# Mixed expert slots of a half and two quarters in a post-norm attention and expert kernel

## The reference, cut to what matters

```python
x = layernorm(x + attn_block(x))       # 8 x 512 tokens of width 256: sparse linear, 16 heads, dense FFN
x = layernorm(x + expert_block(x))

def expert_block(x):                   # 8 experts, E x (256 -> 1024 -> 256), one expert a token
    aff = x @ centroids.T
    assign = argmax(aff, axis=1)
    alpha = sigmoid(aff[assign])
    h = relu(layernorm(x, ln_g[e], ln_b[e]) @ w1[e].T + b1[e])
    y = x + h @ w2[e].T + b2[e]        # e = assign of the token
    return alpha * y + (1 - alpha) * x
```

## Time and profile before

| | |
|---|---|
| median of 3 runs | 870.22 us (870.16 to 870.26) |
| the profiled execution | 868.88 us, of which the trace spans 867.1 us |
| PE busy | 849.4 us (98%) |
| DVE, ACT, POOL busy | 460.1 (53%), 338.2 (39%), 288.9 us (33%) |
| mean granted TensorE clock | 0.995 of 2.4 GHz |
| HBM read, written | 76.33 MB, 11.49 MB |

### The profile page before, as it was taken

One profiled execution on the slowest core, in us unless ns is written; L12 is line 12 of the kernel. 1 busy time (PEld: TensorE's weight loads), 2 busy tenths in 40 slices (PEclk: granted clock), 3 DMA queues, 4 the chain that ended last, 5 costly groups with the idle time before them and its releaser, 6 DMA issues.

```text
span 867.1 us, 19050 instructions
## 1 busy us (share of the span) xinstructions
PE 849.4 (98%) x7078; PEld 570.2 (66%) x7078; DVE 460.1 (53%) x1374; ACT 338.2 (39%) x650; POOL 288.9 (33%) x404
## 2 busy tenths in 40 slices
PE   8999999999999999999999999999999999999994
PEld 4545576476467467557557647779989767667673
DVE  5465355256257347346448526525785556556552
ACT  1443415424432432631532442414233545454540
POOL 3503021422242061061152133415555444444422
PEclk9999999999999999999999999999999999999998
DMA  6501100020020020020002104224638876767820
GB/s 245 183 3 31 43 2 1 26 74 1 26 74 1 26 73 2 26 74 1 27 26 99 50 1 135 99 74 149 208 126 289 284 254 232 264 235 245 287 76 12
DMA packets 37697, 88.53 MB, mean 102 GB/s; under 512 B 13411, under 2 KB 26596, under 8 KB 30310
## 3 DMA queue, kind: packets, MB, share of 16 engines
q1 hardware_dynamic: 32118, 75.40, 25.5%
q0 software_dynamic: 5056, 11.37, 4.1%
q10 hardware_dynamic: 432, 0.54, 0.2%
HBM read 76.33 MB, written 11.49 MB: 101 GB/s over the span
## 4 chain that ended last, share of the span: by engine, by line
PE 92%; DVE 4%; POOL 1%; issue 1%; ACT 1%; DMA 1%; POOLq 0%; DVEq 0%; ACTq 0%
PE ps L580 13%; PE ps L586 12%; PE ps L673 9%; PE ps L691 9%; PE ps L527 8%; PE ps L551 7%; PE ps L738 5%; PE ps L713 4%; PE ps L499 3%; PE ps L559 3%; PE ps L426 3%; PE ps L447 3%; PE ps L455 3%; PE ps L389 2%; PE ps L723 1%; PE ps L659 1%
## 5 line engine op out<-in xcount | busy, mean ns | idle before, releaser
L586 PE MATMUL ps<-ff2T,hT 128*128 128x256 f32 x512 | 121.0, 384 | 0.2 <-ACT hT L1479 0.2
L580 PE MATMUL ps<-xT,ff1T 128*128 128x512 f32 x256 | 118.8, 604 | 0.1
L1487 ACT ACTIVATE arena<-ps 128x1536 f32<-128x1536 f32 (+3 forms) x49 | 65.1, 1328 | 127.5 <-DVE arena L985 126.9
L586 PEld LDWEIGHTS ps<-ff2T,hT 128*128 128x128 f32 x512 | 94.3, 190 | 16.3 <-issue 3.4
L985 DVE SCALAR_TENSOR_TENSOR arena<-ps,arena 128x512 f32<-128x512 f32 (+4 forms) x59 | 44.9, 767 | 105.7 <-PE ps L527 63.2
L691 PE MATMUL ps<-w_sb,arena 128*128 x400 | 95.8, 383 | 0.0
L691 PEld LDWEIGHTS ps<-w_sb,arena 128*128 128x128 f32 x400 | 72.2, 190 | 17.3 <-issue 9.5
L580 PEld LDWEIGHTS ps<-xT,ff1T 128*128 128x128 f32 x256 | 45.6, 190 | 52.2 <-issue 47.9
L527 PE MATMUL ps<-arena 32*128 32x512 f32 (+7 forms) x896 | 73.0, 434 | 1.7 <-ACT hT L1004 1.2
L1557 ACT ACTIVATE arena<-ps,arena 128x128 f32<-128x128 f32 (+1 forms) x94 | 34.3, 429 | 98.5 <-PE ps L659 98.5
L1792 POOL DMA_INDIRECT out_y<-arena,ids x36 | 37.3, 1035 | 87.4 <-DVE arena L1281 80.1
(11 more groups left out here) (209 smaller groups left out, 1487.5 us busy)
## 6 DMA issues: line engine op xcount, KB each, us to landing
arena<-in_w SPq DMA_DIRECT2D x24, 1024.0 KB, 5.4
hT<-in_w SPq DMA_DIRECT2D x14, 1024.0 KB, 6.7
wts<-in_w SPq DMA_DIRECT2D x9, 1024.0 KB, 5.4
w_sb<-in_w SPq DMA_DIRECT2D x8, 1024.0 KB, 5.1
token_store<-x SPq DMA_DIRECT2D x8, 520.0 KB, 3.6
arena<-in_x SPq DMA_DIRECT2D x8, 512.0 KB, 3.9
arena<-in_epack SPq DMA_DIRECT2D x25, 134.0 KB, 3.6
slot_table<-padid POOLq DMA_DIRECT2D x4, 576.0 KB, 6.0
```

The lines of the kernel that those rows point to most:

```text
L580: last = eng.matmul(ps[:, 6 + m % 2, :], ff1T[:, kd, m * P:(m + 1) * P], xT3[:, kd, :], start=kd == 0, stop=kd == KD - 1)
L586: last = eng.matmul(quarter(6, t), hT[:, m, t * P:(t + 1) * P], ff2T[:, m, :], start=m == 0, stop=m == FM - 1)
L1487: eng.activation(o, i, ACT.Relu).then_inc(s_sa, 1)
```

## The change

Left-over rows are handed out in units of 64 and 32 instead of 64 alone. A mixed slot now has three parts: a half (64 rows) and two quarters (32 rows each), each of its own expert. With that the rows fit in 34 slots: the same 25 full ones and 9 mixed ones instead of 11. The mixed slots are 14, 16, 18, 21, 23, 25, 28, 30 and 32.

- PE: the layers of a mixed slot run in four column strips of 32 (the half's two strips read the same weights): 16 products instead of 8 in layer 1 and 32 instead of 16 in layer 2, each half as wide in its stationary operand.
- First weights: three ring buffers a mixed slot (3 MB) instead of two, in the same ring of six.
- Second weights: all three parts are copied by ACT (three copies of 128x2048 instead of one), in four fixed places in turn.
- Parameters: six DMAs for a mixed slot instead of four, ids three instead of two. `slot_act_x_T` has six operations instead of four.
- Hidden units of a mixed slot: DVE adds the biases for both halves of them with four broadcast operations, then ACT and DVE take one relu each, instead of eight operations on either engine.
- Tables: four instead of three, the last one built in step 9 of DVE; the first mixed ids wait for all four.
- SP's order in a step becomes: first weights of j, parameters of j, ids of j+3.
- Two pairs of SBUF tensors are laid side by side so that they can serve as weight copies.

```diff
-QT = P // 2
+QT = P // 4
 NQ = P // QT
+PART_ROWS = (slice(0, 2 * QT), slice(2 * QT, 3 * QT), slice(3 * QT, P))
+NP = len(PART_ROWS)
+PART_OF = (0, 0, 1, 2)
...
-MIXED = {j: (j - N_EARLY) // 2 for j in range(N_EARLY + 1, N_TILE, 2)}
+MIXED = {N_EARLY + i: (i + 1) * N_MIX // N_LATE for i in range(N_LATE) if (i + 2) * N_MIX // N_LATE > (i + 1) * N_MIX // N_LATE}
...
-N_TAB = (N_EARLY, N_FULL - N_EARLY, NQ * N_MIX)
+N_TAB = (N_EARLY, N_FULL - N_EARLY, N_MIX, 2 * N_MIX)
+UNIT = (P, P, 2 * QT, QT)
...
-            w1_of[j] = [queue.pop(0) for _ in range(NQ if j in MIXED else 1)]
+            w1_of[j] = [queue.pop(0) for _ in range(NP if j in MIXED else 1)]
...
 # mixed_pe_layer1
                     for q in range(NQ):
-                        last = eng.matmul(ps[half_rows(q), b0 + i, :], sxT[u][:, kd, half_rows(q)],
-                                          w1_ring[w1_of[j][q]][:, c:c + S], start=kd == 0, stop=kd == KD - 1,
+                        last = eng.matmul(ps[quarter_rows(q), b0 + i, :], sxT[u][:, kd, quarter_rows(q)],
+                                          w1_ring[w1_of[j][PART_OF[q]]][:, c:c + S], start=kd == 0, stop=kd == KD - 1,
...
 # mixed_pe_layer2
-            eng.wait_ge(m_w2, MIXED[j] + 1)
+            eng.wait_ge(m_w2, NP * (MIXED[j] + 1))
...
 # mixed_dve_hidden
+            for k, (turned, done) in enumerate(((m_Ta, m_add), (m_Tb, m_add2))):
+                eng.wait_ge(turned, i + 1)
...
+                eng.tensor_tensor(shT[u][:, f, 0:2 * QT], src[:, :, 0:2 * QT], c[:, e].unsqueeze(2).broadcast_to([P, 4, 2 * QT]),
+                                  ALU.add)
+                eng.tensor_tensor(shT[u][:, f, 2 * QT:P].rearrange("p f (q c) -> p f q c", c=QT),
+                                  src[:, :, 2 * QT:P].rearrange("p f (q c) -> p f q c", c=QT),
+                                  quarters[:, e, :].unsqueeze(3).broadcast_to([P, 4, NP - 1, QT]), ALU.add).then_inc(done, 1)
+            eng.wait_ge(m_add2, i + 1)
+            eng.tensor_scalar(shT[u][:, 4:FM, :], shT[u][:, 4:FM, :], 0.0, None, ALU.max).then_inc(p_hTd, 1)
...
 # dve_program
                 if j == 8:
                     dve_find_experts(eng, 2)
                     dve_slot_table(eng, 2)
+                    dve_count_tiles(eng, 3)
+                if j == 9:
+                    dve_place_tiles(eng, 3)
+                    dve_find_experts(eng, 3)
+                    dve_slot_table(eng, 3)
...
 # act_program
-                if j == N_EARLY:
-                    mixed_act_second_weights(eng, 0)
-                if j in MIXED and MIXED[j] + 1 < N_MIX:
-                    mixed_act_second_weights(eng, MIXED[j] + 1)
+                if j in MIXED:
+                    mixed_act_weights(eng, NP * MIXED[j] + 1)
+                elif j == N_EARLY or j - 1 in MIXED and MIXED[j - 1] + 1 < N_MIX:
+                    mixed_act_weights(eng, NP * (MIXED[j - 1] + 1) if j - 1 in MIXED else 0)
...
                 if j + 1 < N_TILE:
                     slot_act_norm(eng, j + 1)
+                if j in MIXED:
+                    mixed_act_weights(eng, NP * MIXED[j] + 2)
...
 # slot_sp_ids
             if MIXED[j] == 0:
-                eng.wait_ge(s_tab, 3)
+                eng.wait_ge(s_tab, len(N_TAB))
...
 # sp_program
-                if XN <= j + 3 < N_TILE:
-                    slot_sp_ids(eng, j + 3)
                 slot_sp_w1(eng, j)
                 slot_sp_ep(eng, j)
+                if XN <= j + 3 < N_TILE:
+                    slot_sp_ids(eng, j + 3)
```

More of the change, by code:

```diff
@@ L375, in turn_of, with quarter_rows, columns_of @@
             return 16 * sum(parts if i in MIXED else 1 for i in range(j % ring, j + 1, ring))
-        def half_rows(q):
+        def quarter_rows(q):
             return slice(q * QT, (q + 1) * QT)
+        def columns_of(part):
+            return EW + 12 * (part - 1) if part else 0
         def pe_keep_warm(eng, bank, count):
@@ L704, in mixed_pe_layer1 @@
             u, b0 = j % UN, 2 * (j % 2)
-            for q in range(NQ):
-                eng.wait_ge(s_w1[w1_of[j][q]], turn_w1[j][q])
+            for p in range(NP):
+                eng.wait_ge(s_w1[w1_of[j][p]], turn_w1[j][p])
             eng.wait_ge(p_xTe, j + 1)
@@ L1552, in slot_act_x_T @@
                 eng.wait_ge(p_l1d, j - UN + 1)
-            for q, rows in enumerate([half_rows(q) for q in range(NQ)] if j in MIXED else [slice(0, P)]):
+            for p, rows in enumerate(PART_ROWS if j in MIXED else (slice(0, P),)):
                 for kd in range(KD):
-                    g, b = q * EW + E_G + kd, q * EW + E_B + kd
+                    g, b = columns_of(p) + E_G + kd, columns_of(p) + E_B + kd
                     last = eng.activation(sxT[u][:, kd, rows], ps[:, 6, kd * P + rows.start:kd * P + rows.stop], ACT.Identity,
@@ L1905, in slot_sp_ids @@
             if MIXED[j] == 0:
-                eng.wait_ge(s_tab, 3)
-            for q in range(NQ):
-                at = half_entry(eng, j, q, 1, NE * N_TOK)
-                eng.dma_start(ids[half_rows(q), j:j + 1], places[bass.ds(at, QT), 0:1],
+                eng.wait_ge(s_tab, len(N_TAB))
+            for p, rows in enumerate(PART_ROWS):
+                at = part_entry(eng, j, p, 1, NE * N_TOK)
+                eng.dma_start(ids[rows, j:j + 1], places[bass.ds(at, rows.stop - rows.start), 0:1],
                               allow_slow_non_contiguous=True).then_inc(d_ids[j % XN], 16)
@@ L1920, in slot_sp_ep @@
                 return
-            for q in range(NQ):
-                row = half_entry(eng, j, q, 2, (NE - 1) * P)
-                eng.dma_start(ep[j % EN][:, q * EW:q * EW + 12], epack[bass.ds(row, P), 0:12],
+            for p, rows in enumerate(PART_ROWS):
+                row, c = part_entry(eng, j, p, 2, (NE - 1) * P), columns_of(p)
+                eng.dma_start(ep[j % EN][:, c:c + 12], epack[bass.ds(row, P), 0:12],
                               allow_slow_non_contiguous=True).then_inc(d_ep[j % EN], 16)
-                eng.dma_start(ep[j % EN][half_rows(q), E_B2:E_B2 + H],
-                              epack[bass.ds(row, QT), E_B2:E_B2 + H]).then_inc(d_ep[j % EN], 16)
+                eng.dma_start(ep[j % EN][rows, E_B2:E_B2 + H],
+                              epack[bass.ds(row, rows.stop - rows.start), E_B2:E_B2 + H]).then_inc(d_ep[j % EN], 16)
         def slot_sp_w1(eng, j):
@@ L1945, in slot_sp_w1 @@
                     eng.wait_ge(s_f2, 2 * NB)
-            for q, u in enumerate(w1_of[j]):
-                row = half_entry(eng, j, q, 2, (NE - 1) * P) if j in MIXED else slot_entry(eng, j, 2, (NE - 1) * P)
+            for p, u in enumerate(w1_of[j]):
+                row = part_entry(eng, j, p, 2, (NE - 1) * P) if j in MIXED else slot_entry(eng, j, 2, (NE - 1) * P)
                 eng.dma_start(w1_ring[u], w1[bass.ds(row, P), :]).then_inc(s_w1[u], 16)
```

153 lines of the change are left out of this document (84 added, 69 removed).

## The result

The changed kernel takes 895.64 us (median of 4 runs, 894.93 to 896.92) beside 870.19 for the kernel before on the same chip: 1.0294 times, with a 95% interval of 1.0277 to 1.0312. The prediction was 865.9 with a range up to 874.5, so both the value and the sign were wrong. The profiled execution spans 893.5 us against 867.1, and the difference of 26.4 us is what has to be explained. Some 1.3 us of it lie between executions and not between kernels, since the profiled execution of the kernel before took 868.88 us, 1.3 under the median of 870.22.

The account below looks back on a forecast made before the run. PE, busy 98%, was taken to bound the kernel: 867.1 - 17.24 + 0.5 + 10.2 + 0.3 + 1.9 = 862.8 us of span, and with 3.1 to the median 865.9 us; 8-in-10 range 856.5 to 874.5.

Parts of the forecast that it names:

- Two slots: PE's path: two mixed slots go at 8.62 us each, 17.24 us off, while the 25 full slots stay.
- Four strips: Mixed slots' layers on PE: four strips run side by side, 0.05 us a slot more, 0.5 us for nine.
- Which slots wait: PE before layer 1: 16, 18, 23, 25, 30 and 32 wait for first weights and parameters, no other mixed slot.
- The wait's size: PE before layer 1: parameters land at 12.0 us, layer 1 starts near 14.2 against 12.44; 1.7 us in six slots, 10.2.
- the second rival: DMA queue before layer 1: loads run at 3.65 us each, waits of 3.1 us a slot, 874.3 us; chance 0.2.
- s: PE's wait before layer 1 in each of the six waiting slots: 1.7 us expected, bounds 1.0 and 3.1.
- The clock: PE in the expert slots: granted clock already at the 2.4 GHz level, so nothing to be had from it.
- 855.7 + 6 s: Whole kernel's time in us, with s as the wait of each of six slots; breaks even at s = 2.4.
- The tables: DVE's table building up to step 9: later normalisation and late first mixed ids, 1.9 us more, bounds 0.6 and 4.
- Who else stands behind this: POOL's gather and DVE's normalisation behind the later ids of j+3: hidden by some 2 us, no cost.
- x_T: ACT's `slot_act_x_T` before layer 1: six operations take 1.77 us; 0.3 us for three mixed slots without the long wait.
- ACT and DVE: Mixed slots: some 3 us more ACT work a pair, DVE within 1 us; both cost 0, bounds 0 and 0.5 a slot.

## Why the prediction was wrong, step by step

- **Two slots, -17.24.** Right: in the version with a wait for each buffer the waits before layer 1 are 6.9 us, its layers 1 take 4.5 us more than 9 x 3.43, and the tables cost 2.6; with two slots saved that gives 867.1 - 17.24 + 6.9 + 4.5 + 2.6 = 863.9 us, and 1.3 for the execution, against a span of 865.6. Without them it could not be under the kernel before.
- **Four strips, +0.5.** Right in kind, short in size: 0.12 us a slot, 1.1 for nine, all of it in layer 1.
- **Which slots wait.** The six named do, 21 and 28 don't. Slot 14 was missed: the distance of its buffers is four slots, but at the start a backlog of other weights and table waits stands before it on SP. I looked at the ring and not at SP's order there, although the rows of 655 to 671 showed that backlog. 3.9 us, and 1.7 more for its slow layer (5.34 against 3.64). With the backlog taken away the wait was 0.34.
- **The wait's size, six times 1.7.** This is the step that failed. PE's work between (12.42 us against 12.44), the starts of SP's issues and ACT's 1.77 were right within 0.2 us. The landing was not. The third load was to land at 11.6 and the parameters 0.4 behind. The forecast took 2.9 us a load from the mean rate of the DMA engines, and that mean was right: 361 GB/s in the window shown, 1.05 MB in 2.9 us. But landings aren't means. The third load landed 11.6 us after the first issue and not 10.7 (the run with parameters first), one parameter DMA behind it landed at 13.2 and not 12.0, and six of them another 1.2 later. From the 4.9 us of a load alone to 11.6 for the third are 3.35 us a load, between the 2.9 taken and the 3.65 of the earlier trace rows, which stood in the prediction as the bound and as the second rival's; I set it aside since gathers shared that window. The 1.2 us for six DMAs stood nowhere.
- **Where the second rival falls short.** It named the mechanism and s = 3.1, and gave 874.3. The waits were 3.45. The other 20 us are mostly the next point and slot 14.
- **The clock.** The prediction read 1.00 in the kernel before and took it that "nothing is to be had from it". There was something to lose. With forecast waits of 1.7 us little might have been lost: in the run with one parameter DMA, waits of 1.72, 1.86, 2.10 and 2.34 us left layer 1 at 3.64. But 2.24 and 2.52 gave 5.34 there, 2.00 gave 5.37 in the run with half the bytes, and in all runs 3 to 6 us gave 4.9 to 6.5. In the kernel after, layer 1 has 44.86 us against 9 x 3.64 = 32.8 at the upper level: 12.1 us for the clock and 1.9 for the strips and for starting behind a wait. The time is not 855.7 + 6 s; somewhere between s of 1.9 and 2.4 each slot adds nearly 2 us at once, just below where the sum breaks even (2.4), so that the second rival should have been priced some 10 us higher (six times 5.34 less 3.64).
- **The tables, +1.9.** 3.1 us by their two waits, or 2.6 more than the 0.5 of the earlier trace rows, inside the bounds of 0.6 to 4.
- **Who else stands behind this, x_T, ACT and DVE.** POOL's 11.9 us stay covered, and the ids' order costs nothing there. No row has PE waiting for copies of second weights in the kernel after.

Put together: 862.8 forecast; 10.5 for the six waits, 3.9 for slot 14, 13.5 for layer 1 (14.0 less the 0.5), 0.7 for the tables and 0.4 for slots 21 and 28 make 891.8, and with the 1.3 between executions 893.1, against a span of 893.5. Of the 29.8 us between the forecast of 865.9 and the measured 895.64, some 21 follow from the one step, the landing: 10.5 of longer waits and 10.4 of the lower clock behind them. Slot 14 has another 5.6.

**What stays open.** What holds a landing back beyond the bytes. The rate of a backlog read by landings was 3.35 to 3.65 us a load, by bytes 2.9. The packets of the kernel after in the two half microseconds from 702 on give a hint: few bytes in many small packets on the queue.

```profile
DMA packets 310, 0.11 MB, mean 230 GB/s; under 512 B 242, under 2 KB 305, under 8 KB 305
...
DMA packets 235, 0.05 MB, mean 94 GB/s; under 512 B 207, under 2 KB 233, under 8 KB 233
```

These are mostly the parameters, and they take the engines a microsecond for 0.16 MB. But the run that took away 336 of their 384 rows of 48 bytes saved nothing (the six DMAs have 512 rows in all, and not the 768 of the expectation above). What of the 1.2 us is the number of DMAs, what their late issues and what the rows was not taken apart. That one of the sixteen engines is behind the others, and a landing waits for it, might explain both; that is a guess, and no run here looks at single engines.

## What to carry to other kernels

When a slot takes several buffers of a ring, let each load wait for its own buffer: the same change with that one edit went from 1.029 to 0.997 times the kernel before. Price a wait behind a backlog by landings of a backlog in the trace and not by the mean rate, and count the queue's issuing engine as a resource with its own busy time. And where PE gets a new wait as long as the ones here, 2 us and more, price it twice, once for itself and once for the layer behind it, which may run at the lower clock.

## What the hardware showed that was not expected

- In the runs of this case every stand of PE before layer 1 of 2.46 us or more (up to 6.06) was followed by a layer 1 of 4.9 to 6.5 us in place of 3.64 (after the 4.06 us of slot 16 its first 3 us ran at the 1.2 GHz level), and none of 1.86 us or less was. In between both were seen: 1.99, 2.00, 2.11 and 2.24 with the loss, 2.10, 2.30 and 2.34 without.
- Six small DMAs in place of one behind 3 MB cost 1.2 us a slot at the landing, for 12 KB more; fewer rows in the same six gave nothing back.
- SP needs about 1.1 us for a DMA whose address it loads from a table, and a pair of slots has 13 to 15, which is by estimate 13 to 15 us in a period of 16.3. In the version with a wait for each buffer SP waits for others only 20.6 of the 165 us from 685 on. The engine that only issues has little time of its own left.
